# Graph network, two layers: layer 0's node MLP in two halves around VectorE sums, and 40-row gathers in the last group

## The reference, cut to what matters

```python
# N = 6250 nodes of 256 numbers, E = 200000 edges sorted by dst
# layer 0
msg = relu(x[src] + edge_attr @ W_edge + b_edge)
agg = segment_sum(msg, dst, num_segments=N)
h = (1.0 + eps) * x + agg
h = relu(h @ W1 + b1) @ W2 + b2
h = relu((h - mean(h, axis=0)) * rsqrt(var(h, axis=0) + 1e-5) * gamma + beta)
x = layernorm(x + h)
# layer 1: graph attention with 4 heads, W, att
x = layernorm(x + attention(x, W, att, src, dst))
```

## Time and profile before

| | us |
|---|---|
| median of three runs | 4175.82 (4168.08 to 4180.40) |
| profiled execution, its own time | 4172.38 |
| its span | 4170.5 |
| POOL busy | 3051.2 (73%) |
| PE busy, PEld busy | 3109.0 (75%), 2384.8 (57%) |
| DVE busy, ACT busy | 2311.8 (55%), 786.9 (19%) |
| mean granted clock of PE, share of full speed | 0.879 |

### The profile page before, as it was taken

One profiled execution on the slowest core, in us unless ns is written; L12 is line 12 of the kernel. 1 busy time (PEld: TensorE's weight loads), 2 busy tenths in 40 slices (PEclk: granted clock), 3 DMA queues, 4 the chain that ended last, 5 costly groups with the idle time before them and its releaser, 6 DMA issues.

```text
span 4170.5 us, 55725 instructions
## 1 busy us (share of the span) xinstructions
PE 3109.0 (75%) x13609; PEld 2384.8 (57%) x13709; DVE 2311.8 (55%) x5835; ACT 786.9 (19%) x1504; POOL 3051.2 (73%) x3229
## 2 busy tenths in 40 slices
PE   6888788898888889988876666566666666666665
PEld 5666666676666667766654445444544544444444
DVE  5444444444444444443466666676766776777776
ACT  2222222222222222222240000010110111111212
POOL 7777777777777777777547777777777777777775
PEclk9999999999999999999987877878777787777887
DMA  5555555545455555454365555555555555555554
GB/s 177 159 155 154 157 154 159 159 149 154 149 164 154 153 151 160 150 160 147 108 160 158 156 157 161 157 162 160 160 161 161 161 160 161 166 160 163 162 167 121
DMA packets 321505, 651.46 MB, mean 156 GB/s; under 512 B 149711, under 2 KB 170425, under 8 KB 321465
## 3 DMA queue, kind: packets, MB, share of 16 engines
q0 software_dynamic: 150528, 414.45, 35.0%
q1 hardware_dynamic: 164448, 230.16, 17.9%
q10 hardware_dynamic: 6489, 6.40, 0.5%
HBM read 637.67 MB, written 13.08 MB: 156 GB/s over the span
## 4 chain that ended last, share of the span: by engine, by line
POOL 29%; PE 20%; issue 19%; DMA 13%; DVEq 8%; DVE 7%; ACT 2%; ACTq 1%; POOLq 1%; SPq 0%
POOL rows L382 29%; PE psum L881 7%; DMA rows<-z_tab,idx 6%; PE psum L870 6%; DMA rows<-in_x,idx 5%; DVEq L747 4%; DVE rows L988 2%; PE psum L867 1%; DVEq L743 1%; PE psum L890 1%; PE psum L925 1%; PE psum L912 1%; PE psum L600 1%; PE psum L917 1%; DVE rows L817 1%
## 5 line engine op out<-in xcount | busy, mean ns | idle before, releaser
L382 POOL DMA_INDIRECT rows<-in_x,idx x1568 | 1510.7, 963 | 536.1 <-issue 451.9
L382 POOL DMA_INDIRECT rows<-z_tab,idx x1568 | 1504.4, 959 | 482.7 <-issue 454.7
L988 DVE TENSOR_TENSOR rows<-rows,psum 128x1024 f32<-128x1024 f32 x392 | 478.6, 1221 | 1153.8 <-DMA rows<-in_x,idx 797.7
L600 PE MATMUL psum<-rows,onehot 128*128 128x260 f32 x3136 | 1045.1, 505 | 41.3 <-issue 41.0
L600 PEld LDWEIGHTS psum<-rows,onehot 128*128 128x128 f32 x3136 | 794.9, 260 | 222.9 <-issue 49.5
L870 PE MATMUL psum<-weights,edge_room 128*128 128x256 f32 x3136 | 816.2, 383 | 6.7 <-issue 2.0
L881 PE MATMUL psum<-rows,onehot 128*128 128x256 f32 x3136 | 784.5, 396 | 0.0
L870 PEld LDWEIGHTS psum<-weights,edge_room 128*128 128x128 f32 x3136 | 607.4, 194 | 161.9 <-issue 9.0
L968 ACT ACTIVATE rows<-rows 128x1024 f32<-128x1024 f32 x392 | 414.3, 1057 | 1496.9 <-DVE rows L988 1496.8
L881 PEld LDWEIGHTS psum<-rows,onehot 128*128 128x128 f32 x3136 | 606.4, 198 | 80.6
L817 DVE TENSOR_TENSOR rows<-rows,psum 128x1024 f32<-128x1024 f32 x392 | 460.9, 1217 | 78.2 <-ACT psum L689 78.2
(11 more groups left out here) (156 smaller groups left out, 1704.5 us busy)
## 6 DMA issues: line engine op xcount, KB each, us to landing
dst_t<-in_dst_jp SPq DMA_DIRECT2D x197, 512.0 KB
edge_room<-in_edge_t SPq DMA_DIRECT2D x196, 512.0 KB, 3.9
rows<-in_x,idx POOLq DMA_INDIRECT x1568
rows<-z_tab,idx POOLq DMA_INDIRECT x1568
z_tab<-edge_room SPq DMA_DIRECT2D x14, 455.0 KB, 6.3
idx<-in_src_idx SPq DMA_DIRECT2D x392, 4.0 KB, 1.6
dst_t<-in_x_t SPq DMA_DIRECT2D x14, 448.0 KB, 5.5
rows<-in_x_t SPq DMA_DIRECT2D x14, 448.0 KB, 5.8
```

Source lines behind the costliest of these rows:

```text
L382: nc.gpsimd.indirect_dma_start(rows[:, u, j, 0:width], None, table, bass.IndirectOffsetOnAxis(ap=idx[:, u, j:j + 1], axis=0)).then_inc(L.r ...
L600: last = pe.matmul(agg_ps[0:WIN, 0:width], onehot[:, hot, j, :], rows[:, u, j, 0:width], start=(j == 0), stop=(j == J - 1))
L988: dve.tensor_tensor(half, half, psum[:, 2 * b:2 * b + 2, :].rearrange("p b (j d) -> p (b j) d", j=2), ALU.add).then_inc(added, 1)
```

## The change

PE no longer multiplies x by (1 + eps) W1. VectorE forms (1 + eps) x + acc in place in `acc`, for one chunk at a time (`add_nodes`, one instruction of 128 partitions by 896 elements, counted by the new semaphore `a_sum`), and PE makes one product of it with W1. The second product of chunk c moves to the turn of chunk c+1, ahead of its first product, and so do its bias and the statistics (two turns later on VectorE). The first product uses banks 2 and 3 and the second one banks 0 and 1. The second product of chunk 12 runs after the last round, ahead of the remaining half sums; the statistics of chunks 11 and 12 are then made on VectorE between the last two windows. The loads of x wait for `a_sum`. PE and ScalarE wait for the loads of the weights ahead of their first group. In both layers the last round of gathers is taken out of POOL's loop (`peeled`), and the gathers of group 195 fetch 40 rows each in place of 128.

```diff
@@ rounds @@
-        def rounds(eng, body, finish_nodes=None, ends=0, begun=False):
+        def rounds(eng, body, finish_nodes=None, ends=0, begun=False, peeled=0):
...
             if finish_nodes is None:
-                return until(0, ROUNDS - 1)
+                until(0, ROUNDS - 1 - peeled)
+                for n in range(ROUNDS - peeled, ROUNDS):
+                    for u in range(RING):
+                        body(n, u, n * RING + u)
+                return
...
+        def filled(g):
+            return -(-(EDGES - (GROUPS - 1) * GROUP) // J) if isinstance(g, int) and g == GROUPS - 1 else P
@@ gather, pass_gathers, single0_gathers @@
-        def gather(L, table, width, u):
+        def gather(L, table, width, u, count=P):
             for j in range(J):
                 nc.gpsimd.indirect_dma_start(
-                    rows[:, u, j, 0:width], None, table,
-                    bass.IndirectOffsetOnAxis(ap=idx[:, u, j:j + 1], axis=0)).then_inc(L.rows_in[u], 16)
+                    rows[0:count, u, j, 0:width], None, table,
+                    bass.IndirectOffsetOnAxis(ap=idx[0:count, u, j:j + 1], axis=0)).then_inc(L.rows_in[u], 16)
...
-                gather(L, table, width, u)
-            rounds(pool, body, begun=begun)
+                gather(L, table, width, u, filled(g))
+            rounds(pool, body, begun=begun, peeled=1)
@@ single0_loads @@
-                sp.wait_ge(a_pe1, HALF * c)
+                sp.wait_ge(a_sum, c)
@@ single0_matmuls @@
-            def finish_nodes(c, at):
-                pe.wait_ge(w1x_ready, 1)
...
+            def first_product(c):
+                pe.wait_ge(a_sum, c + 1)
                 for m in range(HALF):
                     for k in range(HALF):
...
+                        last = pe.matmul(banks[2 + m][:, 0:CHUNK], w1[:, k, m * P:(m + 1) * P],
+                                         acc[:, k, bass.ds(c * CHUNK, CHUNK)], start=(k == 0), stop=(k == HALF - 1))
+                    last.then_inc(a_pe1, 1)
+
+            def second_product(c):
+                pe.wait_ge(a_act1, 2 * c + 2)
                 for m in range(HALF):
                     for k in range(HALF):
...
+                        last = pe.matmul(banks[m][:, 0:CHUNK], w2[:, k, m * P:(m + 1) * P], x_in[1][:, k, :],
                                          start=(k == 0), stop=(k == HALF - 1))
                 last.then_inc(a_pe2, 1)
+
+            def finish_nodes(c, at):
+                pe.wait_ge(added, 2 * at + 1)
+                with pe.If(c > 0):
+                    second_product(c - 1)
+                pe.wait_ge(added, 2 * at + 2)
+                first_product(c)
                 pe.wait_ge(a_act2, c + 1)
+                pe.wait_ge(a_act1, 2 * c + 2)
 
             def finish_last(c, at):
...
+                first_product(c)
+                pe.wait_ge(a_act2, c + 1)
+                second_product(c)
 
             pe.wait_ge(bias_ready, 1)
+            pe.wait_ge(const_in, 16 * WEIGHT_LOADS)
             c0 = rounds(pe, body, finish_nodes)
+            pe.wait_ge(added, 2 * GROUPS - 1)
+            with pe.If(c0 > 0):
+                second_product(c0 - 1)
@@ single0_act @@
-            c0 = rounds(act, body, mlp_act(act, 0, 2))
+            def first_relu(c):
+                for k in range(HALF):
+                    act.wait_ge(a_pe1, 2 * c + k + 1)
+                    act.activation(x_in[1][:, k, :], banks[2 + k][:, 0:CHUNK], ACT.Relu,
+                                   bias=cols[:, 0, k:k + 1]).then_inc(a_act1, 1)
...
+            def second_bias(c):
+                act.wait_ge(a_pe2, c + 1)
+                for k in range(HALF):
+                    ins = act.activation(node_x[:, k, bass.ds(c * CHUNK, CHUNK)], banks[k][:, 0:CHUNK],
+                                         ACT.Identity, bias=cols[:, 1, k:k + 1])
+                ins.then_inc(a_act2, 1)
+
+            def finish_nodes(c, at):
+                with act.If(c > 0):
+                    act.reg_mov(before, c - 1)
+                    second_bias(act.snap(before, min_val=0, max_val=CHUNKS - 2))
+                first_relu(c)
...
+            act.sem_inc(a_act2, 1)
+            c0 = rounds(act, body, finish_nodes)
+            with act.If(c0 > 0):
+                act.reg_mov(before, c0 - 1)
+                second_bias(act.snap(before, min_val=0, max_val=CHUNKS - 2))
             copy_window((GROUPS - 2) % RING, GROUPS - 2, 2 * GROUPS + 1)
             copy_window((GROUPS - 1) % RING, GROUPS - 1, 2 * GROUPS + 3)
-            last_nodes(act, mlp_act(act, 0, 2), c0)
+            last_nodes(act, finish_last, c0)
@@ single0_vector @@
-            c0 = rounds(dve, body, mlp_dve(dve, 1))
...
+            def add_nodes(c):
+                chunk = acc[:, :, bass.ds(c * CHUNK, CHUNK)]
+                dve.wait_ge(a_in, 16 * c + 16)
+                dve.scalar_tensor_tensor(chunk, x_in[0], eps1[:, 0:1], chunk, ALU.mult, ALU.add).then_inc(a_sum, 1)
...
+            def earlier_statistics(c, back):
+                with dve.If(c > back - 1):
+                    dve.wait_ge(a_act2, c + 2 - back)
...
+            def finish_nodes(c, at):
+                add_nodes(c)
+                earlier_statistics(c, 2)
...
             add_window((GROUPS - 3) % RING, GROUPS - 3, 2 * GROUPS + 1)
             add_window((GROUPS - 2) % RING, GROUPS - 2, 2 * GROUPS + 3)
+            earlier_statistics(c0, 2)
+            earlier_statistics(c0, 1)
             add_window((GROUPS - 1) % RING, GROUPS - 1, 2 * GROUPS + 4)
-            last_nodes(dve, mlp_dve(dve, 2), c0)
+            last_nodes(dve, finish_last, c0)
@@ tensor, after layer 0 @@
-            pe.wait_ge(a_act2, CHUNKS)
+            pe.wait_ge(a_act2, CHUNKS + 1)
```

More of the change, by code:

```diff
@@ L262, in build @@
         half_done, added, bias_ready = sem("half_done"), sem("added"), sem("bias_ready")
+        a_sum = sem("a_sum")
         def two(name):
@@ L855, in body @@
                 pool.sem_inc(passed, 1)
-                gather(layer0, t["x"], D, u)
-            rounds(pool, body, begun=True)
+                gather(layer0, t["x"], D, u, filled(g))
+            rounds(pool, body, begun=True, peeled=1)
         def single0_matmuls(pe):
@@ L915, in finish_nodes @@
+            def second_product(c):
+                pe.wait_ge(a_act1, 2 * c + 2)
                 for m in range(HALF):
                     for k in range(HALF):
-                        last = pe.matmul(banks[m][:, 0:CHUNK], w1[:, k, m * P:(m + 1) * P],
-                                         acc[:, k, bass.ds(c * CHUNK, CHUNK)], start=False, stop=(k == HALF - 1))
-                    last.then_inc(a_pe1, 1)
-                pe.wait_ge(added, 2 * at + 2)
-                for m in range(HALF):
-                    for k in range(HALF):
-                        if m == 0:
-                            pe.wait_ge(a_act1, 2 * c + k + 1)
-                        last = pe.matmul(banks[2 + m][:, 0:CHUNK], w2[:, k, m * P:(m + 1) * P], x_in[1][:, k, :],
+                        last = pe.matmul(banks[m][:, 0:CHUNK], w2[:, k, m * P:(m + 1) * P], x_in[1][:, k, :],
@@ L932, in finish_last @@
-                pe.wait_ge(a_in, 16 * c + 16)
-                pe.wait_ge(a_act2, c)
-                for m in range(HALF):
-                    for k in range(HALF):
-                        pe.matmul(banks[m][:, 0:CHUNK], w1x[:, k, m * P:(m + 1) * P], x_in[0][:, k, :],
-                                  start=(k == 0), stop=False)
-                pe.wait_ge(layer0.group_done, GROUPS)
-                for m in range(HALF):
-                    for k in range(HALF):
-                        last = pe.matmul(banks[m][:, 0:CHUNK], w1[:, k, m * P:(m + 1) * P],
-                                         acc[:, k, bass.ds(c * CHUNK, CHUNK)], start=False, stop=(k == HALF - 1))
-                    last.then_inc(a_pe1, 1)
@@ L944, in finish_last @@
-                for m in range(HALF):
-                    for k in range(HALF):
-                        if m == 0:
-                            pe.wait_ge(a_act1, 2 * c + k + 1)
-                        last = pe.matmul(banks[2 + m][:, 0:CHUNK], w2[:, k, m * P:(m + 1) * P], x_in[1][:, k, :],
-                                         start=(k == 0), stop=(k == HALF - 1))
-                last.then_inc(a_pe2, 1)
+                first_product(c)
+                pe.wait_ge(a_act2, c + 1)
+                second_product(c)
@@ L978, in body, with finish_last @@
                 relu(u, g, 1)
-            c0 = rounds(act, body, mlp_act(act, 0, 2))
+            def first_relu(c):
[3 more added lines that the diff above has]
+                                   bias=cols[:, 0, k:k + 1]).then_inc(a_act1, 1)
+            before = act.alloc_register("chunk_before")
+            def second_bias(c):
[9 more added lines that the diff above has]
+                first_relu(c)
+            def finish_last(c, at):
+                first_relu(c)
+                second_bias(c)
+            act.wait_ge(const_in, 16 * WEIGHT_LOADS)
```

(4 more changed lines are left out.)

19 lines of the change are left out of this document (13 added, 6 removed).

## The result

The changed kernel takes 4124.95 us (median of five runs, 4121.54 to 4126.39) and the kernel before 4174.94 (4168.08 to 4180.40): a ratio of 0.9879, 95% interval 0.9867 to 0.9890. The profiled execution took 4123.64 us, its span is 4121.5.

What follows compares the result with a forecast made beforehand. POOL, with 29% of the chain, was taken as the bound, its gathers filling nearly all of layer 0. Terms -24.1 - 5.5 + 6 - 0.9 = -24.5 against 4172.4 gave 4148 us, range 4129 to 4168.

Steps and rivals of the forecast that it cites:

- The 40-row gathers: group 195's gathers on POOL: 0 won in layer 0, 0.9 us in layer 1; bounds 0 to 7.7 us a layer.
- rival D: gathers of 40 rows cost POOL as much as those of 128; only the 0.9 is lost, 4149 us; chance 0.02.
- The MLP part: node MLP turns and layer 0's end: -24.1 from late starts, -5.5 from gaps behind them, +6 at the end.
- rival A: PE's shorter rest keeps the clock up; all 54 us of stalls go but 13 x 0.95; 4135 us, chance 0.17.
- late starts and held gathers, layer 0: POOL's 13 late gathers at MLP turns: 24.1 us won, 0.95 lost per gather held by VectorE's sum; 5.5 more from gaps behind.
- layer 0's end: work once hidden moves behind the last gathers of layer 0: costs 6 us, bounds 3.1 and 9.
- the three large ones: the three largest of POOL's 13 late starts in layer 0: 2.2 us won on each, 6.6 together.
- follow-up gaps: seven gaps of 1.57 us before the gather behind a late one, layer 0: 0 to 11 us won, 5.5 taken.
- The port: VectorE's new sum with two SBUF inputs holds a POOL gather until it ends: 0.95 us lost each time.
- Layer 1's end: VectorE's wait of 0.96 for layer 1's last rows: 0.9 us won by gathering 40 rows.
- Priced at nothing: wait for weights before the first group, SP's wait on a_sum, VectorE's sum and statistics: no cost.
- C: rival: leaving each new If block on PE or ScalarE costs 4.14 us a turn; +32, 4204 us, chance 0.09.

Runs made afterwards that it cites:

- after_128: kernel after with 128 rows again in group 195 of both layers, peeled round kept; 4144.35 us, ratio 0.9932 to the kernel before.
- after_again: the kernel after, unchanged, run once more in a later job; 4122.16 us, ratio 0.9880 to the kernel before.
- the two branches: layer 1's two copies under a run-time If, in the kernel after; 40-row gathers only in the executed one 4122.41 us, only in the other 4145.70.
- short_not_taken: kernel after with 40-row gathers only in the branch of layer 1 that is not executed; 4145.70 us, ratio 0.9946 to the kernel before.
- tail_split: kernel after with layer 0's end reordered and VectorE's sum as two instructions of 448 elements; 4112.69 us, ratio 0.9867 to the kernel before.
- tail_all: kernel after with chunk 12's second product behind the last transpose, statistics of chunks 11 and 12 behind chunk 13's sum; 4116.93 us, ratio 0.9865.

## Why the prediction was wrong, point by point

**The step that failed is "The 40-row gathers".** It asked only what the sixteen short gathers cost, gave layer 0 nothing and layer 1 0.9, and held every other gather at the 0.963 of the earlier trace rows. The short gathers do bring nothing themselves (rival D was right on that: most take 0.90 to 0.93 us, against 0.95). But the 128-row gathers, 1560 a layer, moved by 11 and 4 ns, and that measured 21.5 us on the kernel before (12.5 to 26.7 by its interval), 22.2 on the kernel after (*after_128* against *after_again*) and 23.3 between the two branches. My bounds for this term, 0 to 7.7 a layer, did not hold it in layer 0 either (1560 x 0.011 = 17 us): they bounded the wrong instructions.

**The MLP part** was forecast at -24.1 - 5.5 + 6 = -23.6 and measured -29.8, with an interval of -22 to -35 that still holds the forecast: by the time alone it is not told from it. The mechanism is right, and the trace shows one size well off; the whole lies halfway to rival A, in which this part is -42 + 6 = -36. By its own steps, from *after_128*:

| term | forecast | measured |
|---|---|---|
| turn, PE back after | 11.2 | 9.9 (10.66 in the kernel after) |
| sum of VectorE | 1.09 | 1.15 |
| held gather, lost each | 0.95 | 0.67 to 0.87 |
| late starts and held gathers, layer 0 | -29.6 | -50.5 + 10.7 = -39.8 |
| layer 0's end | +6 | +6.3 |

The spans of the two profiled executions differ by 30.5. The rest beside -39.8 and +6.3 had no term: 1.6 more ahead of group 4, 0.9 less within layer 1, and 2.4 more behind its last gather (33.2 against 30.8).

The mis-sized term is what POOL still sees of a turn. I took 2.2 off each old stall, so that the three large ones kept 1.7 to 4.6 each, and gave the follow-up gaps their middle. In *after_128* all went but 2.8 us. Two things go together here. The clock keeps its upper level in more of the turns, which was the reason behind rival A: in the 17 us behind a turn's start the level of 1.2 GHz is on record in all twelve later turns before, for 5.0 to 5.5 us in the three with the largest stalls, and in four of the twelve in *after_128*; PE's rest before it is back is 3.76 at the turn of 1369 before and 3.06 at that of 1359 here. And no gap of 1.57 is left in that trace, only the three of 0.95; *short_not_taken* has one of 1.57 and six of the twelve turns with the lower level. How much each brings was not separated.

In the kernel after the late starts are 16.7 us and not 2.8; over all traces of the changed MLP on chips of the first kind they are 12.1 (*after_again*) to 16.7 with short gathers, and 2.8 and 8.8 without. The shorter gathers bring POOL to the critical group sooner, the turn's PE work comes 0.75 later within it (1354.40 - 1350.06 = 4.3 to the first product, 1362.68 - 1359.10 = 3.6 in *after_128*), and the first turn at the low clock adds 3.05. For that turn the prediction said that it waits for the same sum as the others and gets the same; that failed, since PE has nothing to do ahead of the sum and its product then runs at the lower level. So a part of what the shorter gathers give in layer 0 is lost again. 9.8 of the 16.7 us are gaps ahead of a group's second gather: two of 1.58 behind a late first one, and four of 1.43 to 1.51 and one of 0.76 without one. No row names their releaser; what the rows show, here and in *tail_split*, is that the gather starts 0.5 to 0.6 us after VectorE has ended the add of a window that stands behind its streak of one-hot matrices (1367.34 + 0.41 = 1367.75, gather at 1368.33).

**The port.** The row won over the rule. The gathers are held beside the new sum, at 1.63 to 1.84 us against 0.95, and less with the sum in halves. The later a gather starts within the sum, the shorter it takes, and it ends about 0.8 us behind the sum: in the kernel after at 1353.18 + 1.80 = 1354.98, the sum at 1353.00 + 1.15 = 1354.15. The Trainium skill, "SBUF — State Buffer", Who interferes with whom, infers that a VectorE tensor_tensor with two SBUF inputs does not keep GpSimd from generating descriptors; taken as a rule for these gathers, as the prediction took it, the traces of this case do not agree. By the rule the first turn's gather would take 0.95; it took 1.79. The gathers also read their indices from SBUF (the `idx` of their rows), which this reading of the rule leaves out; no run tells whether that or the writing of descriptors is what waits.

**Layer 0's end**: right in sum, and in its parts but one. The statistics took 0.66 + 2.21 = 2.9 us, as forecast; PE's idle 4.37 and the product at 1.2 GHz (5.68 in place of 3.17) had no term. **Layer 1's end**: against the kernel before the 0.9 is not there, 30.8 to 30.7; VectorE's wait for the last rows has gone from the timeline, and what took its place was not followed up. Among the changed kernels the end is 33.2 and 33.3 us with 128 rows (*after_128*, *short_not_taken*) and 30.4 to 32.2 with 40, so a gain of the forecast's size or more isn't ruled out. **Priced at nothing**: the wait for the weights and the peeled round. The first gather of group 4 starts at 49.87 before and at 50.40 after, 49.72 in *after_again*: nothing to be told. **C**, dear blocks, is refuted: PE's rest before it is back, 3.05, is less than the 3.96 in the earlier trace rows.

**Still open**: what it is that the short gathers leave behind, why layer 0's own do not leave it, why layer 0 gains more than layer 1, and what makes the gaps ahead of a second gather. That it is carried from one execution to the next is concluded from the order of the work, not seen. Open too are the 3 ns by which changed code without short gathers is slower on the slower chips. I did not try a program that executes layer 1's other branch, short gathers in another place of layer 1, or a first execution by itself.

The version that beats both kernels is *tail_all*, 4116.93 us, ratio 0.9865, 5 us under *after_again*; *tail_split* has 4112.69 and 0.9867 on another chip, so its extra edit brings nothing that these runs tell.

## What to carry to other kernels

Where one engine issues thousands of equal instructions and bounds the kernel, a few nanoseconds on each outweigh whole stalls: compare the median length of that instruction in both traces before explaining anything else. Time the parts of a combined change apart, also the part that seems to be worth nothing. When PE loses a piece of its work ahead of a wait, ask how long it then stands still and at which clock it goes on; work that is pulled into such a wait pays twice.

## What the runs showed of the hardware that I had not expected

- In every kernel whose executed layer 1 ends with gathers of fewer than 128 rows (40 or 112) the 128-row gathers of the whole program are shorter, by their medians: 957 to 946 ns in layer 0 and to 953 in layer 1. On slower chips they are 949 and 957, against 960 in both layers of the changed kernels without them and 957 in both of the kernel before.
- An indirect gather costs POOL nearly the same whatever its rows: mostly 0.90 to 0.93 us for 40, 0.93 for 112, 0.95 to 0.96 for 128, and 0.30 behind each.
- A sum on VectorE of two SBUF inputs holds a gather that starts beside it until the sum has ended; two instructions of half the size let it through between them (1.18 to 1.38 in *tail_split* in place of up to 1.84 in *tail_all*). A gather that starts just ahead of the sum isn't held (0.95).
- The same program took 4169 to 4175 us on some chips and 5389 or 5455 on others, with POOL's share of the chain at 29% on the former and 0% on the latter.
